# State-space stage: GpSimd multiplies a unit's four states by C in one instruction, not in two of two states each

## The chip, the cores and the metric

One NeuronCore of a Trainium2 chip runs the whole program. The metric is the device time of one execution in microseconds (us). Five engines run their own instruction streams and meet at semaphores: TensorE (PE in the profile), VectorE (DVE), ScalarE (ACT), GpSimd (POOL) and SyncE (SP, which issues DMAs).

## What is computed

A model of two layers on 2 x 4096 tokens of width 512. The change is in its first block, a selective state-space block (Mamba), which is cut here to what the scan needs:

```
h   = silu(causal_conv4(layernorm(x) @ in_proj_hidden))          # 1024 channels
dt, B, C = rms-normed parts of h @ x_proj_w                      # B, C: 16 states per token
dt  = softplus(dt @ dt_proj_w + dt_proj_b)
s_t = exp(dt_t * A) * s_(t-1) + dt_t * h_t * B_t                 # per channel and state
y_t = sum over the 16 states of s_t * C_t
x   = x + ((y + h * D) * silu(gate)) @ out_proj_w
```

A mixing matmul, a linear-attention layer and a routed spline layer follow. They are a stage of their own, which begins when the first has ended.

## The kernel before

**Tiling.** The state-space stage (`mamba_block`) goes through 16 chunks: 8 blocks of T = 512 tokens for each of 2 batch rows. A chunk holds 1024 channels x 16 states x 512 tokens. Channels lie in 8 groups of 128 partitions and states in 4 quarters of 4. A **unit** is one group with one quarter: 128 channels x 4 states x 512 tokens, so 32 units a chunk and 512 in all. The loop over units is `for k in range(U)` in the body of each engine. I call its turn number k of a chunk **step k**.

**What each engine does for unit k.** The order on each engine is written out by hand.

- TensorE, `b_product(k)` (line 737): 16 small matmuls make dt * h * B for the four states in the four PSUM banks `BU`. There is one `BU`, so it waits for `scan_done`, until all four scans of unit k-1 have read it.
- ScalarE (line 501): four exponentials write exp(dt * A) into the slot `s[k % 4]`. They wait for `sum_done`, which tells that the slot's former unit has been summed.
- VectorE (lines 651 to 656): four scans, one for each state, in place in `s[k % 4]`. Then comes `piece(k)`, a part of the work that prepares the next chunk (convolution, norm, softplus, gating), and then a small reduce, which saves the last column and signals `state_saved`.
- GpSimd (line 335): waits for `state_saved` of unit k, multiplies `s[k % 4]` in place by `Cb`, which is C broadcast to all partitions, and signals `z_ready`. It does so in two instructions of two states each.
- TensorE, `y_sum(k_even, part)` (line 754): 8 matmuls with the identity add the products into the PSUM banks `Y`. A call handles two states of an even unit and of the odd unit behind it. `part` 0 takes states 0 and 1, `part` 1 states 2 and 3.
- SyncE (line 219) loads the next `Cb` when `z_ready` tells that the units so far are multiplied.

**The order on TensorE.** In step k it runs `b_product(k)`, then larger pieces for the next or the previous chunk (`before(k)` and `main(k)`: transposes and projections into `PJ`), and one call `sums(k)`. In odd steps (but for k = 11) `sums(k)` comes right after `b_product(k)`. In even steps it comes last, so that `b_product(k+1)` stands right behind it; in step 12 eight transposes stand between. In an even step `sums(k)` is part 0 of the units k-2 and k-1. In an odd step it is part 1 of the units k-3 and k-2. Its wait counts product instructions:

```
pe.wait_ge(z_ready, c * 2 * U + 2 * k - 1 if part == 0 else c * 2 * U + 2 * (k - 1))
```

With two signals a unit, the value 2k-1 is reached when GpSimd has done all of unit k-2 and the first half of unit k-1.

Of the kernel before, what the change touches and what calls it, by code (L numbers as in the profile page):

```python
# [9 lines left out]
ALU = mybir.AluOpType  # L10
# [4 lines left out]
T = 512  # L15
# [6 lines left out]
def wait(eng, sem, value):  # L22

    if not isinstance(value, int) or value > 0:
        eng.wait_ge(sem, value)
# [33 lines left out]
def mamba_block(nc, x, in_w, chan, xproj_w, dt_w, out_w, eye, tokmask, x1):  # L59
# [9 lines left out]
    U = G * NQ  # L69
# [3 lines left out]
    NCH = BATCH * NI  # L73
    SLOTS = 4
# [6 lines left out]
    with ctx:  # L81
        def sb(name, shape, dt=F32):
            return ctx.enter_context(nc.sbuf_tensor(name, shape, dt))
# [4 lines left out]
        def sem(name):  # L88
            return ctx.enter_context(nc.semaphore(name))
# [21 lines left out]
        s = [sb(f"s{i}", [P, 4, T]) for i in range(SLOTS)]  # L111
        Cb = [sb(f"Cb{i}", [P, 4 * T]) for i in range(2)]
# [33 lines left out]
        z_ready, sum_done, y_ready = sem("z_ready"), sem("sum_done"), sem("y_ready")  # L146
# [57 lines left out]
        def _(sp):  # L204
            def held(sem_, value):

                wait(sp, sem_, value)
                sp.sem_inc(sp_steps, 1)
# [8 lines left out]
            def load_c(q, slot):  # L217
                src = bc[slot][4 * (q % NQ):4 * (q % NQ) + 4, :].rearrange("(o n) t -> o (n t)", o=1)
                sp.dma_start(Cb[q % 2][:], src.to_broadcast([P, 4 * T])).then_inc(c_loaded[q % 2], 16)
# [5 lines left out]
            def load_x(ring_, use, period, b_next, i_next, half):  # L225
                held(*ring_.emptied(use, period))
                sp.dma_start(xt[:], x_v[b_next, i_next, :, 2 * half:2 * half + 2, :]).then_inc(x_loaded, 16)
# [6 lines left out]
            def load_res(i_prev, b_prev, c_prev, j):  # L234

                held(x1_stored[j % 2], 16 * (c_prev * 2 + j // 2))
                sp.dma_start(res[:, j % 2, :], x_v[b_prev, i_prev, :, j, :]).then_inc(res_loaded[j % 2], 16)

            def store_x1(i_prev, b_prev, c_prev, j):
                held(x1_ready, c_prev * NT + j + 1)  # L240
                sp.dma_start(x1_v[b_prev, i_prev, j], res[:, j % 2, :]).then_inc(x1_stored[j % 2], 16)

            def body(i, b, c, first, last):
                i_prev, b_prev, c_prev = (i, 0, c - 1) if b else (i - 1, 1, c - 1)
                i_next, b_next = (i + 1, 0) if b else (i, 1)
                for k in range(U):
                    if k == 0:
                        if not last:
                            held(spread_ready, NQ * (c + 1))
                            if first:  # L250
                                load_x(ahead, ("xT", 3), 0, b_next, i_next, 0)
                            else:
                                load_x(steady, ("xT", 3), c - 1, b_next, i_next, 0)
                        if not first:
                            held(bc_stored, 16 * (c + 1))
                            load_res(i_prev, b_prev, c_prev, 0)
                            load_res(i_prev, b_prev, c_prev, 1)
                    if k % 2 == 0:
                        held(z_ready, c * 2 * U + 2 * k)
                        if k // 2 + 1 < U // 2:  # L260
                            load_c(k // 2 + 1, b)
                        elif not last:
                            held(bc_stored, 16 * (c + 2))
                            load_c(0, 1 - b)
                    if not first:
                        if k == 4:
                            store_x1(i_prev, b_prev, c_prev, 0)
                        if k == 6:
                            load_res(i_prev, b_prev, c_prev, 2)
                        if k == 7:  # L270
                            store_x1(i_prev, b_prev, c_prev, 1)
                        if k == 9:
                            load_res(i_prev, b_prev, c_prev, 3)
                        if k == 11:
                            store_x1(i_prev, b_prev, c_prev, 2)
                        if k == 12:
                            store_x1(i_prev, b_prev, c_prev, 3)
                    if k == 9 and not last:
                        load_x(steady, ("xT", 1), c, b_next, i_next, 1)
                    if k == 29 and not last:  # L280
                        store_bc(steady, c, 1 - b)
# [9 lines left out]
        @block.gpsimd  # L291
        def _(pool):
            nc.gpsimd.memset(minus_half[:], -0.5)
            nc.gpsimd.memset(state[:], 0.0)
            nc.gpsimd.memset(hist[:], 0.0)
            pool.drain().then_inc(consts_ready, 1)

            def ln_power(c_next, half):
                wait(pool, stats_ready, 2 * c_next + half + 1)
                nc.gpsimd.tensor_tensor(rstd[:], ve[:], minus_half[:, 0:2], ALU.pow).then_inc(rstd_ready, 1)  # L300

            def ssm_power(c_next):
                wait(pool, ssq_ready, c_next + 1)
                nc.gpsimd.tensor_tensor(rssm.rearrange("p j n -> p (j n)"), ssq.rearrange("p j n -> p (j n)"),
                                        minus_half[:], ALU.pow).then_inc(rssm_ready, 1)

            def spread_b(c_next, nq):
                pool.wait_ge(ssm_ready, c_next + 1)
                lo = RANK + 4 * nq
                nc.gpsimd.tensor_tensor(spread[:, nq], mask[:].unsqueeze(1).unsqueeze(3).to_broadcast([P, TB, 32, 4]),  # L310
                                        ssm[:, :, lo:lo + 4].unsqueeze(2).to_broadcast([P, TB, 32, 4]),
                                        ALU.mult).then_inc(spread_ready, 1)

            ln_power(0, 0)
            ln_power(0, 1)
            ssm_power(0)
            pool.wait_ge(small_loaded, 48)
            for nq in range(NQ):
                spread_b(0, nq)

            def body(i, b, c, first, last):
                for k in range(U):
                    if k == 2 and not last:
                        ln_power(c + 1, 0)
                    if k == 10 and not last:
                        ln_power(c + 1, 1)
                    if k == K_SUMS and not last:
                        ssm_power(c + 1)
                    q = k // 2
                    if k % 2 == 0:  # L330
                        wait(pool, c_loaded[q % 2], 16 * (c * (U // 4) + (q % (U // 2)) // 2 + 1))
                    wait(pool, state_saved, c * U + k + 1)
                    for part in range(2):
                        pair = s[k % SLOTS][:, 2 * part:2 * part + 2, :].rearrange("p n t -> p (n t)")
                        nc.gpsimd.tensor_tensor(pair, pair, Cb[q % 2][:, 2 * part * T:2 * part * T + 2 * T],  # L335
                                                ALU.mult).then_inc(z_ready, 1)
                    if k == 0 and not first:
                        wait(pool, dbu_ready, c * U)
                        spread_b(c, 3)
                    if k in (28, 29, 30) and not last:  # L340
                        nq = k - 28
                        wait(pool, dbu_ready, c * U + 26 + 2 * nq)
                        spread_b(c + 1, nq)

            periods(pool, body)

        @block.scalar
# [317 lines left out]
        def _(pe):  # L665
# [115 lines left out]
            def body(i, b, c, first, last):  # L781
                def sums(k):
                    part = k % 2
                    k_even = (k - part - 2) % U
                    if k < 2 and first:
                        return
                    if k_even % UP == 0 and part == 0:
                        wait(pe, y_ready, c * G + 2 * (k_even // UP))
                        pe.sem_inc(pe_steps, 1)
                        skip_product(k_even // UP, b)  # L790
                    pe.wait_ge(z_ready, c * 2 * U + 2 * k - 1 if part == 0 else c * 2 * U + 2 * (k - 1))
                    pe.sem_inc(pe_steps, 1)
                    y_sum(k_even, part)

# [49 lines left out]
                for k in range(U):  # L844
                    if k % UP == 0:
                        p = k // UP
# [17 lines left out]

            periods(pe, body)
            for part in range(2):
                pe.wait_ge(z_ready, NCH * 2 * U - 1 + part)
                y_sum(U - 2, part)
            pe.wait_ge(y_ready, G * NCH)
            for j in range(NT):  # L870
# [1020 lines left out]
```

## Time and profile before

| | us |
|---|---|
| median of 3 runs | 5543.72 (5543.46 to 5544.86) |
| the profiled execution, its own time | 5545.57 |
| its span, first to last instruction | 5543.6 |

The span begins with some 120 us of loads and the first chunk's preparation. The scans run from 123.2 to about 3793 us, and the second stage takes the rest. A steady chunk takes some 231 us. The chunk read below is the eighth. Its last step before (k = 31 of the seventh) ends at 1732.6 us, and its steps 4, 12, 16, 22 and 28 are looked at.

How to read it: "busy" is time in which an engine executed something. The time named in square brackets in front of an arrow is how long the engine stood idle before the row, and behind the arrow is the instruction that ended the wait. In the timeline, equal instructions that follow each other are one row with their count. TensorE runs an fp32 matmul as two passes here, so `y_sum` shows as x16 and `b_product` as x32. Ends of matmuls are modelled, so I go by their starts.

### The profile page before, as it was taken

To read this page: it belongs to the slowest core of one execution; us is meant where nothing else is said; L and a number is where in the kernel's file an instruction comes from. 1 tells how busy PE (TensorE), PEld (TensorE's weight loads), DVE (VectorE), ACT (ScalarE), POOL (GpSimd) and SP (SyncE) were. 2 spreads that over 40 slices of the span, in tenths; PEclk is the share of its full clock that TensorE was granted. 3 is DMA by queue.
4 is the path that set the end of the run, shared out by engine and by line. 5 is a ranking of instruction groups with operands and counts; after the bars stand their busy time and mean duration, and the time that the engine had idled before them with its cause. 6 is when DMAs were issued, how large, how long until landed. Compare 5 with 4: busy or idle time off the path is not lost. (4 is left out here: it accounts for less than half of the span.)

```text
span 5543.6 us, 108449 instructions
## 1 busy us (share of the span) xinstructions
PE 4955.6 (89%) x41157; PEld 2941.5 (53%) x41157; DVE 4611.2 (83%) x7532; ACT 2636.9 (48%) x4244; POOL 3148.7 (57%) x1611
## 2 busy tenths in 40 slices
PE   6899999999999999999999999974899999999922
PEld 3354444454445444454444444432688888888822
DVE  3988889888898888988889888884688888888888
ACT  3655656556565565655656556551233333333300
POOL 1676766767667676676766767662244444434323
PEclk9999999999999999999999999987899999999955
DMA  2222222212222222222222222223110000101034
GB/s 82 81 96 73 100 79 90 96 73 100 81 89 96 73 100 84 85 97 73 100 85 85 96 73 100 81 88 133 37 31 28 29 29 28 31 26 31 22 124 140
DMA packets 139999, 422.20 MB, mean 76 GB/s; under 512 B 38368, under 2 KB 39904, under 8 KB 106592
## 3 DMA queue, kind: packets, MB, share of 16 engines
q1 hardware_dynamic: 136672, 411.75, 21.1%
q8 instruction: 337, 5.52, 0.4%
q10 hardware_dynamic: 2816, 3.51, 0.2%
q14 instruction: 174, 1.43, 0.1%
HBM read 361.99 MB, written 53.22 MB: 75 GB/s over the span
## 5 line engine op out<-in xcount | busy, mean ns | idle before, releaser
L335 POOL TENSOR_TENSOR s<-s,Cb 128x1024 f32<-128x1024 f32 x1024 | 2395.0, 2360 | 1081.9 <-DVE state L656 1070.4
L651 DVE TENSOR_TENSOR_SCAN s<-s,state,BU 128x512 f32<-128x512 f32 x2048 | 2452.9, 1260 | 423.4 <-PE BU L737 387.1
L501 ACT ACTIVATE s<-dt,ch 128x512 f32<-128x512 f32 x2048 | 1305.6, 712 | 776.3 <-PE Y L754 774.7
L754 PE MATMUL Y<-s,ident 64*64 64x512 f32 x8192 | 1010.7, 609 | 78.5 <-POOL s L335 77.6
L683 PE MATMUL PJ<-xnT,w_in 128*128 128x512 f32 x2048 | 946.9, 606 | 9.0 <-ACT dtuT L367 5.7
L737 PEld LDWEIGHTS BU<-spread,dtuT 32*128 32x128 f32 x16384 | 512.4, 189 | 528.8 <-DVE s L651 403.2
L737 PE MATMUL BU<-spread,dtuT 32*128 32x128 f32 x16384 | 610.9, 286 | 146.4 <-DVE s L651 141.0
L683 PEld LDWEIGHTS PJ<-xnT,w_in 128*128 128x128 f32 x2048 | 370.1, 190 | 479.0 <-issue 424.2
L754 PEld LDWEIGHTS Y<-s,ident 64*64 64x64 f32 x8192 | 279.1, 134 | 572.8 <-issue 535.2
L728 PE MATMUL PJ<-w_out,u 128*128 128x512 f32 x1024 | 471.7, 604 | 8.3 <-ACT xnT L371 6.7
L728 PEld LDWEIGHTS PJ<-w_out,u 128*128 128x128 f32 x1024 | 184.5, 189 | 242.9 <-issue 225.3
L1103 POOL TENSOR_TENSOR x1t<-x1t,bias_b 128x512 f32<-128x512 f32 x64 | 82.8, 1294 | 397.4 <-DVE xa L1286 397.4
L544 DVE SCALAR_TENSOR_TENSOR u<-hid,ch,u 128x512 f32<-128x512 f32 x384 | 287.6, 749 | 19.1
L694 PE MATMUL PJ<-w_xp,u 128*128 128x160 f32 x1024 | 253.0, 404 | 9.6 <-issue 6.5
L694 PEld LDWEIGHTS PJ<-w_xp,u 128*128 128x128 f32 x1024 | 243.1, 329 | 27.2 <-issue 20.8
L1108 POOL TENSOR_TENSOR xf<-xf,gamma_b 128x512 f32<-128x512 f32 x64 | 81.5, 1273 | 305.3 <-DVE xf L1475 305.3
L1484 DVE TENSOR_TENSOR scm<-bank,decay 128x512 f32<-128x512 f32 x256 | 159.0, 684 | 71.1 <-PE bank L1593 71.1
L1554 PE MATMUL bank<-w_high_o,aTs 128*128 128x512 f32 x512 | 179.9, 412 | 0.0
L1116 POOL TENSOR_TENSOR qk_all<-rc,rs 128x512 f32<-128x512 f32 x64 | 82.1, 1283 | 172.1 <-DVE rs L1502 172.1
L367 ACT COPY dtuT<-PJ 128x512 f32<-128x512 f32 x128 | 68.8, 587 | 231.8 <-PE PJ L723 231.8
L1554 PE MATMUL bank<-w_high_f,xaT 128*128 128x512 f32 x512 | 177.1, 407 | 1.5 <-DVE xaT L1291 1.4
L1291 DVE TENSOR_TENSOR xaT<-bank,xaT 128x512 fp32r<-128x512 f32 x64 | 44.2, 691 | 161.2 <-ACT xaT L1158 161.2
(219 smaller groups left out, 7171.7 us busy)
## 6 DMA issues: line engine op xcount, KB each, us to landing
Cb<-bc SPq DMA_DIRECT2D x256, 1024.0 KB, 4.8
res<-in_x SPq DMA_DIRECT2D x64, 256.0 KB, 4.8
x<-res SPq DMA_DIRECT2D x64, 256.0 KB, 5.0
x1t<-x SPq DMA_DIRECT2D x64, 256.0 KB, 2.6
out<-r_t SPq DMA_DIRECT2D x64, 256.0 KB, 2.0
xt<-in_x SPq DMA_DIRECT2D x31, 512.0 KB, 5.7
x_all<-out SPq DMA_DIRECT2D x16, 512.0 KB, 4.2
scm<-out SPq DMA_DIRECT2D x16, 512.0 KB, 4.6
```

The source lines that it names most:

```text
L335: nc.gpsimd.tensor_tensor(pair, pair, Cb[q % 2][:, 2 * part * T:2 * part * T + 2 * T], ALU.mult).then_inc(z_ready, 1)
L501: nc.scalar.activation(s[k % SLOTS][:, n, :], dt[p % 2][:, gi, :], ACT.Exp, scale=ch[:, 2 * p + gi, 7 + 4 * nq + n:8 + 4 * nq + n]).then_i ...
L544: last_ = nc.vector.scalar_tensor_tensor(out, h_[:, tap:tap + T], ch[:, m, tap:tap + 1], out, ALU.mult, ALU.add)
L651: nc.vector.tensor_tensor_scan(s[k % SLOTS][:, n, :], s[k % SLOTS][:, n, :], BU[:, n::4], state[:, b, k, n:n + 1], ALU.mult, ALU.add).then ...
L683: last_ = nc.tensor.matmul(bank[:], w_in[:, kb, lo:lo + P], xnT[:, kb, :], start=(kb == 0), stop=(kb == KB - 1))
L694: last_ = nc.tensor.matmul(bank[:, tb % 2 * SP_:(tb % 2 + 1) * SP_], by_block(u[slot][:, g, :])[:, tb], w_xp[:, g, :], start=(g == 0), sto ...
L728: last_ = nc.tensor.matmul(bank[:], u[slot][:, g, j * P:(j + 1) * P], w_out[:, g, :], start=(g == 0), stop=(g == G - 1))
L737: last_ = nc.tensor.matmul(BU[:, i * T:(i + 1) * T].rearrange("p (t b n) -> p b t n", b=TB, n=4)[:, tb], dtuT[rows, gi, tb, :], spread[row ...
L754: last_ = nc.tensor.matmul(Y[r][y_rows(r, gi), :], ident[rows, rows], s[(k_even + gi) % SLOTS][rows, n, :], start=False, stop=(n == 3 and ...
L1103: nc.gpsimd.tensor_tensor(x1t[s_][:], x1t[s_][:], bias_b[:], ALU.add).then_inc(S["x1b_ready"], 1)
L1484: nc.vector.tensor_tensor(scm[:, r, :, :].rearrange("p k n -> p (k n)"), bank(f"sc{r}")[:], decay[:, r, :, :].rearrange("p k n -> p (k n)" ...
L1554: last_ = nc.tensor.matmul(b_[:], src[part][:, k, :], wt, start=(k == 0 and i == 0), stop=(k == KB - 1 and i == 2))
```

## The change

The product of a unit by C becomes one instruction over 2048 elements a partition. `z_ready` counts once a unit. The waits of TensorE and SyncE are rewritten for that count. In even steps TensorE now waits for all of unit k-1, since a half of a unit no longer has a signal of its own. In odd steps it waits for unit k-2, as before.

```diff
--- before.py
+++ after.py
@@ -256,7 +256,7 @@
                     if k % 2 == 0:
-                        held(z_ready, c * 2 * U + 2 * k)
+                        held(z_ready, c * U + k)
@@ -330,10 +330,8 @@
                     wait(pool, state_saved, c * U + k + 1)
-                    for part in range(2):
-                        pair = s[k % SLOTS][:, 2 * part:2 * part + 2, :].rearrange("p n t -> p (n t)")
-                        nc.gpsimd.tensor_tensor(pair, pair, Cb[q % 2][:, 2 * part * T:2 * part * T + 2 * T],
-                                                ALU.mult).then_inc(z_ready, 1)
+                    whole = s[k % SLOTS][:].rearrange("p n t -> p (n t)")
+                    nc.gpsimd.tensor_tensor(whole, whole, Cb[q % 2][:], ALU.mult).then_inc(z_ready, 1)
@@ -788,7 +786,7 @@
-                    pe.wait_ge(z_ready, c * 2 * U + 2 * k - 1 if part == 0 else c * 2 * U + 2 * (k - 1))
+                    pe.wait_ge(z_ready, c * U + k - (part == 1))
                     pe.sem_inc(pe_steps, 1)
                     y_sum(k_even, part)
@@ -864,7 +862,7 @@
             for part in range(2):
-                pe.wait_ge(z_ready, NCH * 2 * U - 1 + part)
+                pe.wait_ge(z_ready, NCH * U)
                 y_sum(U - 2, part)
```

GpSimd, the first chunk from step 2 on (`rstd` and `xt` are its small instructions for the next chunk's norms, `spread` the broadcast of B). Before:

```order
L300 TENSOR_TENSOR rstd<-ve,minus_half 128x2
L335 TENSOR_TENSOR s<-s,Cb 128x1024 x16
L300 TENSOR_TENSOR rstd<-ve,minus_half 128x2
L335 TENSOR_TENSOR s<-s,Cb 128x1024 x32
L304 TENSOR_TENSOR xt<-xt,minus_half 128x12
L335 TENSOR_TENSOR s<-s,Cb 128x1024 x6
```

And now:

```order
L300 TENSOR_TENSOR rstd<-ve,minus_half 128x2
L334 TENSOR_TENSOR s<-s,Cb 128x2048 x8
L300 TENSOR_TENSOR rstd<-ve,minus_half 128x2
L334 TENSOR_TENSOR s<-s,Cb 128x2048 x16
L304 TENSOR_TENSOR xt<-xt,minus_half 128x12
L334 TENSOR_TENSOR s<-s,Cb 128x2048 x3
```

Nothing changes its place. Every pair of products has become one instruction of twice the size.

TensorE in step 12 of a steady chunk, with its waits (L716 is a projection of `dt`, L676 the transposes of the next input; ISA and REGISTER_ALU are instructions of its sequencer). Before:

```order
L716 MATMUL PJ<-dtnT,w_dt 128x512 [waits proj_taken_dve_steady] x2
L791 REGISTER_ALU
L754 MATMUL Y<-s,ident 64x512 [waits z_ready]
L754 MATMUL Y<-s,ident 64x512 x7
L25 REGISTER_ALU
L25 REGISTER_ALU [waits xn_ready]
L676 MATMUL PJ<-ident,xt 128x128 [waits proj_taken_act_steady]
```

And now:

```order
L714 MATMUL PJ<-dtnT,w_dt 128x512 [waits proj_taken_dve_steady] x2
L752 MATMUL Y<-s,ident 64x512 [waits z_ready]
L752 MATMUL Y<-s,ident 64x512 x7
L25 REGISTER_ALU
L25 REGISTER_ALU [waits xn_ready]
L674 MATMUL PJ<-ident,xt 128x128 [waits proj_taken_act_steady]
```

The matmuls keep their order. The register instruction of line 791, which computed the wait's value, is gone (two line numbers less are the change's own lines), and the wait on `z_ready` has the same place but stands for another event.

## Rows read from the trace of the kernel before

**Rows 1.** The page's busy times: engine, busy us (share of span), instructions.

```profile
PE 4955.6 (89%) x41157; PEld 2941.5 (53%) x41157; DVE 4611.2 (83%) x7532; ACT 2636.9 (48%) x4244; POOL 3148.7 (57%) x1611
```

**Rows 2.** The page's costliest groups: busy us, mean ns | idle before, releaser.

```profile
L335 POOL TENSOR_TENSOR s<-s,Cb 128x1024 f32<-128x1024 f32 x1024 | 2395.0, 2360 | 1081.9 <-DVE state L656 1070.4
L651 DVE TENSOR_TENSOR_SCAN s<-s,state,BU 128x512 f32<-128x512 f32 x2048 | 2452.9, 1260 | 423.4 <-PE BU L737 387.1
...
L754 PE MATMUL Y<-s,ident 64*64 64x512 f32 x8192 | 1010.7, 609 | 78.5 <-POOL s L335 77.6
```

**Rows 3.** Timeline, step 12: start us, duration us, engine, instruction [idle before].

```profile
1816.12 4.68 POOL L335 TENSOR_TENSOR s<-s,Cb 128x1024 f32<-128x1024 f32 x2 [2.06 <-DVE state L656]
...
1818.62 1.95 PE L754 MATMUL Y<-s,ident 64*64 64x512 f32 x16 [1.11 <-POOL s L335]
1820.50 1.09 PE L676 MATMUL PJ<-ident,xt 128*128 128x128 f32 x8
1821.52 1.17 PE L737 MATMUL BU<-spread,dtuT 32*128 32x128 f32 x32
...
1822.85 4.80 DVE L651 TENSOR_TENSOR_SCAN s<-s,state,BU 128x512 f32<-128x512 f32 x4 [1.32 <-PE BU L737]
```

**Rows 4.** Timeline, step 4 and the start of step 5.

```profile
1762.27 4.68 POOL L335 TENSOR_TENSOR s<-s,Cb 128x1024 f32<-128x1024 f32 x2 [1.65 <-DVE state L656]
...
1765.30 1.95 PE L754 MATMUL Y<-s,ident 64*64 64x512 f32 x16
1767.18 1.17 PE L737 MATMUL BU<-spread,dtuT 32*128 32x128 f32 x32
...
1768.91 4.79 DVE L651 TENSOR_TENSOR_SCAN s<-s,state,BU 128x512 f32<-128x512 f32 x4
```

**Rows 5.** Timeline, step 16 and the start of step 17.

```profile
1848.02 1.95 PE L754 MATMUL Y<-s,ident 64*64 64x512 f32 x16 [0.18 <-POOL s L335]
...
1850.20 1.17 PE L737 MATMUL BU<-spread,dtuT 32*128 32x128 f32 x32 [0.23 <-DVE s L651]
...
1852.83 3.61 DVE L651 TENSOR_TENSOR_SCAN s<-s,state,BU 128x512 f32<-128x512 f32 x3
```

**Rows 6.** Timeline, step 22 to the start of step 24.

```profile
1894.62 1.95 PE L754 MATMUL Y<-s,ident 64*64 64x512 f32 x16 [0.48 <-POOL s L335]
1896.79 1.17 PE L737 MATMUL BU<-spread,dtuT 32*128 32x128 f32 x32 [0.23 <-DVE s L651]
...
1905.16 1.17 PE L737 MATMUL BU<-spread,dtuT 32*128 32x128 f32 x32
...
1906.48 2.45 DVE L651 TENSOR_TENSOR_SCAN s<-s,state,BU 128x512 f32<-128x512 f32 x2 [2.31 <-PE BU L737]
```

**Rows 7.** Timeline, step 28 and the start of step 29.

```profile
1940.47 1.95 PE L754 MATMUL Y<-s,ident 64*64 64x512 f32 x16 [1.43 <-POOL s L335]
...
1943.03 1.17 PE L737 MATMUL BU<-spread,dtuT 32*128 32x128 f32 x32 [0.61 <-DVE s L651]
...
1944.35 2.45 DVE L651 TENSOR_TENSOR_SCAN s<-s,state,BU 128x512 f32<-128x512 f32 x2 [1.19 <-PE BU L737]
```

**Rows 8.** One line's instructions on GpSimd: duration ns min/median/max, first and last start.

```profile
L1108 POOL TENSOR_TENSOR xf<-xf,gamma_b x64: 1261/1273/1303, 3973.9 to 5277.2; 128x512 f32<-128x512 f32 x64
L300 POOL TENSOR_TENSOR rstd<-ve,minus_half x32: 695/696/711, 20.0 to 3424.3; 128x2 f32<-128x2 f32 x32
```

**Rows 9.** Busy times in a stretch: from:to, us, PE busy (instructions), granted clock, DMA.

```profile
230.00:3660.00 3430.00, 3255.25 (x28232) 1.00 0.25 88
...
187.00:190.00 3.00, 3.00 (x40) 0.50 0.02 5
```

**Rows 10.** Timeline, TensorE: first chunk, last chunk, and step 18 of the eighth.

```profile
186.84 2.09 PE L737 MATMUL BU<-spread,dtuT 32*128 32x128 f32 x32 [3.04 <-DVE s L651]
...
3740.99 3.69 PE L754 MATMUL Y<-s,ident 64*64 64x512 f32 x16 [1.45 <-POOL s L335]
...
1864.14 1.95 PE L754 MATMUL Y<-s,ident 64*64 64x512 f32 x16 [0.65 <-POOL s L335]
```

## The prediction, made before the result was known

> **What bounds the kernel now.** I read the page's busy times first. TensorE is busy for 89% of the span, VectorE for 83% and GpSimd for 57% [rows 1], so GpSimd as a whole has time to spare and a cheaper product buys nothing by itself. The costliest groups say who waits for whom. VectorE's scans stand idle for 423.4 us, and 387.1 of them end with `b_product`. GpSimd's 1081.9 us of idle time end with the reduce that saves the state, and `y_sum` waited for GpSimd for only 78.5 us [rows 2]. So the state-space stage is set by a loop of TensorE and VectorE: the scans of a unit end, `b_product` of the next unit runs, its scans start. GpSimd hangs on that loop through one thread: in even steps `y_sum` stands ahead of the next `b_product` on TensorE. The timeline shows how tight this thread is. In step 12 the two products start at 1816.12, 4.68 us for both. With 2.36 for one [rows 2] the first half ends at 1818.48, and `y_sum` starts at 1818.62, 0.14 later, while the second half still runs [rows 3]. This shape, `y_sum` on the heels of the first half, is there in six even steps of a steady chunk: 12, 16, 18, 20, 22 and 28.
>
> **What the change costs, part by part.**
>
> *The product.* Two instructions of 1024 elements go, one of 2048 comes. The trace has none of that size. From 512 to 1024 elements the time grows from 1.273 [rows 8] to 2.360 [rows 2], 1.087 for 512. Two more such steps give 2.360 + 2 x 1.087 = 4.53 us. The long end is the pair as it is, 4.68 [rows 3]. For the short end, all 0.696 us of the two-element instruction [rows 8] would be overhead that is paid once less: 3.98. I take 4.53, the value nearest to the rows of this same operation. GpSimd gains 0.15 us a unit, which lies in its idle time and costs or brings nothing.
>
> *The signal.* In an even step `y_sum` could start when half of unit k-1 was multiplied. Now it starts 0.14 after the whole. Where it followed the first half, it comes 4.53 - 2.36 = 2.17 us later. What is queued behind it on TensorE is `b_product` of the next unit, and VectorE's scans wait for that. Three things can cover the 2.17: work ahead of `y_sum` that ends later than the signal anyway, idle time of TensorE between `y_sum` and `b_product`, and a scan that starts later than `b_product`'s result because VectorE still has its piece to do. `y_sum` holds TensorE for 1.88 us (1765.30 to 1767.18 [rows 4]), and a scan can start 1.33 after the start of its `b_product` (1821.52 to 1822.85 [rows 3]).
> - Step 12: only eight transposes stand between, TensorE isn't idle, and the scans wait for `b_product` [rows 3]. No cover: 2.17.
> - Step 16: `b_product` starts at 1850.20, 0.30 after `y_sum` lets go; the scan starts at 1852.83, 1.30 later than it could [rows 5]. 2.17 - 0.30 - 1.30 = 0.57. The convolutions on VectorE are that cover. Steps 18 and 20 read alike: three times 0.57 = 1.71.
> - Step 22: idle 1896.79 - 1896.50 = 0.29. Then TensorE runs without a gap to the `b_product` of step 24 at 1905.16, for which VectorE waits 2.31 us [rows 6]. So all that is left arrives there: 1.88.
> - Step 28: idle 1943.03 - 1942.35 = 0.68, and the scan waits for `b_product` [rows 7]: 1.49.
> - Step 4: `y_sum` now starts at 1765.30, held by the projections. The product's new end is 1762.27 + 4.53 = 1766.80, so the sum moves to 1766.94, by 1.64. The scan has 0.40 of cover (1768.91 against 1768.51) [rows 4], but TensorE finds no idle time in the next two steps and hands the rest over there: 1.6.
> - The other even steps: most have a `y_sum` that starts late enough behind larger work, and I put 0.5 on the lot.
>
> Sum of the waits: 2.17 + 1.71 + 1.88 + 1.49 + 1.6 + 0.5 = 9.35 us a chunk, 150 us in 16 chunks.
>
> *TensorE's clock.* Today it is granted 1.00 from 230 to 3660 us, thus 2.4 GHz throughout [rows 9]. In the first chunk, where TensorE has less to do, it stood idle for 3.04 us, and then the `b_product` at 186.84 took 2.09 us [rows 10] instead of 1.17 [rows 3]; the granted clock from 187 to 190 is 0.50, which is 1.2 GHz [rows 9]. In the last chunk a `y_sum` behind 1.45 us of idle time took 3.69 instead of 1.95 [rows 10], 1.74 more. The change makes the idle time ahead of `y_sum` longer: 1.11 + 2.17 = 3.28 in step 12 [rows 3], 1.43 + 2.17 = 3.60 in step 28 [rows 7], 0.65 + 2.17 = 2.82 in step 18 [rows 10], 0.48 + 2.17 = 2.65 in step 22 [rows 6]. Two of these are longer than the 3.04 that went ahead of a fall. So I expect falls in every steady chunk: surely those two, and of the two or three stretches between 2.3 and 2.9 half. That is 3.5 falls, each of which costs one `y_sum` at half speed, 1.74, in places whose cover is spent already: 6.1 us a chunk. The first and the last chunk fall today, so 14 are counted: 85 us. The Trainium skill, TensorE: Matmul & The Clock Gate, Part 1, says the same in general: an idle array is throttled, and activity releases it. By that rule the sum is 235; by this trace's steady stretch alone, in which no clock fell, it would be 150.
>
> *What costs nothing.* SyncE's wait stands for the same event as before. The odd steps wait for the same product as before, one step old. One register instruction a step goes from TensorE's sequencer, which works ahead while matmuls run; if it were never hidden, it would give back less than the 0.14 between signal and sum. The exponentials wait for the sums of odd steps, which move only as `b_product` does; the scans waited for `b_product` in 387.1 of their 423.4 idle us [rows 2], so there is little that late exponentials held up. The Trainium skill, GPSIMD Engine Reference, section 2.1, speaks for the change: every Pool instruction pays a software dispatch of tens of cycles. By that rule 512 dispatches are saved; they lie in GpSimd's idle time, and the sum stays what it is.
>
> Sum against the profiled execution: 5545.57 + 150 + 85 = 5780.6. It lies 1.85 above the median, so the forecast for the median is 5543.72 + 235 = 5779.
>
> **The rivals.**
> - *The clock holds.* The idle stretches grow, but TensorE is busy enough around them, and it stays at 2.4 GHz, as it does today in the whole steady stretch. For it: 3255 of those 3430 us are busy [rows 9]. Against it: 3.60 and 3.28 are longer than 3.04. Then only the waits count: 5694. With the short product, 3.98 instead of 4.53, each of seven steps gains 0.55, 3.9 a chunk and 62 in all: 5632. With the long one, 4.68, they lose 0.15 each, 17 in all.
> - *The wait is covered.* If VectorE's pieces covered the later `b_product` in all steps as in step 16, a chunk would lose some 0.5 us and the kernel 8: 5552, within 0.2%. Against it: in steps 12, 24 and 28 to 29 the scans wait for `b_product` today [rows 3, 6, 7].
> - *Faster: the big product is as quick as one half.* If GpSimd's time hung on the instruction and not on its elements, the whole unit would be ready when its first half is today. The point is 2.36 us. Below it the even sums start earlier, and what is to be had is at most the 78.5 us in which `y_sum` waited for GpSimd [rows 2]; at 1.9 us, 0.46 in steps 12, 22 and 28, that is 1.4 a chunk and 22 in all: 5522. Against it: 1273 ns for 512 elements and 2360 for 1024.
> - *More falls.* All five stretches of step 12, 16, 18, 22 and 28 fall, 5 x 1.74 = 8.7 a chunk, 122 in all, with the long product 17 more: 5544 + 150 + 122 + 17 = 5833.
>
> **How the numbers follow.** The waits with falls of the clock, some 5750 to 5835, get 0.70; the waits with a clock that holds 0.26; covered 0.02; faster 0.02. The range goes from 5680, which takes in the clock that holds with a product somewhat shorter than I think (5694 - 14), to 5840, just above all falls with the long product. A measurement here can tell about 0.2%, 11 us, from no change. Faster by more than that: 0.02. Within: 0.02. Slower: 0.96.
>
> **What would show it.** Right: line 334 with 512 instructions of some 4.5 us; in step 12 `y_sum` 0.14 after the product's end, and VectorE's idle time ahead of the scans up from 423 us by more than 100; a steady chunk of some 246 us instead of 231; a granted clock below 1.00 from 230 to 3660 us, with `y_sum` rows of over 3 us. Clock wrong: those rows stay at 1.95 and the clock at 1.00, with a chunk of 240 us. The second stage should keep its length. The forecast fails altogether if the scans of steps 13, 24 and 29 start no later behind their predecessors than now, or if the product takes less than 3 us.

## The result, and the profile after

| | before | after |
|---|---|---|
| median, us | 5544.29 (4 runs, 5543.46 to 5545.29) | 5792.06 (4 runs, 5781.93 to 5794.45) |
| ratio | | 1.0442, 95% interval 1.0427 to 1.0458 |
| profiled execution, its own time | 5545.57 | 5781.93 |
| its span | 5543.6 | 5780.1 |
| stretch of the scans, from the timeline | 123.2 to 3789.8 | 122.0 to 4027.7 |

The change makes the kernel 4.4% slower: 247.8 us by the medians, where 235 were forecast. The profiled execution of the changed kernel is the fastest of its four, 10.1 us below their median, so the two profiles are only 236.4 us apart. All of that lies in the state-space stage: its scans take 3905.7 us instead of 3666.6, 239.1 more, and the rest of the program is 2.6 us shorter.

The page's busy times, as in [rows 1]:

```profile
PE 5026.5 (87%) x41157; PEld 2974.3 (51%) x41157; DVE 4610.1 (80%) x7532; ACT 2639.1 (46%) x4244; POOL 3073.2 (53%) x1099
```

VectorE and ScalarE do the same work as before in a longer span. GpSimd has 512 instructions less and is busy for 75.5 us less, 0.15 for each unit. TensorE has the same number of instructions and is busy for 70.9 us more: some of them ran slower.

The page's costliest groups, which answer to [rows 2] (busy us, mean ns | idle before, releaser):

```profile
L334 POOL TENSOR_TENSOR s<-s,Cb 128x2048 f32<-128x2048 f32 x512 | 2319.6, 4530 | 1389.7 <-DVE state L654 1386.0
...
L649 DVE TENSOR_TENSOR_SCAN s<-s,state,BU 128x512 f32<-128x512 f32 x2048 | 2453.9, 1260 | 663.4 <-PE BU L735 636.0
...
L752 PE MATMUL Y<-s,ident 64*64 64x512 f32 x8192 | 1066.1, 638 | 311.5 <-POOL s L334 311.3
```

`y_sum` waits for GpSimd 311.3 us instead of 77.6. The scans wait for `b_product` 636.0 us instead of 387.1, which is 248.9 more, the size of the loss. The matmuls of `y_sum` have a mean of 638 ns instead of 609.

Step 12 of the eighth chunk in the timeline, which answers to [rows 3] (start us, duration, engine, instruction, idle before in square brackets):

```profile
1917.78 4.52 POOL L334 TENSOR_TENSOR s<-s,Cb 128x2048 f32<-128x2048 f32 x1 [2.21 <-DVE state L654]
...
1922.45 3.64 PE L752 MATMUL Y<-s,ident 64*64 64x512 f32 x16 [3.28 <-POOL s L334]
1926.03 1.09 PE L674 MATMUL PJ<-ident,xt 128*128 128x128 f32 x8
1927.05 1.17 PE L735 MATMUL BU<-spread,dtuT 32*128 32x128 f32 x32
...
1928.38 4.80 DVE L649 TENSOR_TENSOR_SCAN s<-s,state,BU 128x512 f32<-128x512 f32 x4 [5.18 <-PE BU L735]
```

The product ends at 1922.30 and `y_sum` starts 0.15 later. It used to start 2.50 after the product's start and now starts 4.67 after it: 2.17 later. TensorE stands idle for 3.28 us instead of 1.11. Then the sum takes 3.64 us instead of 1.95, since the clock has fallen. The scans behind it waited for 5.18 us instead of 1.32, and 3.86 is 2.17 + 1.69.

Steps 18 (with the `b_product` of step 19) and 28 (with that of step 29) of the same chunk, from the same timeline:

```profile
1972.61 2.65 PE L752 MATMUL Y<-s,ident 64*64 64x512 f32 x16 [2.37 <-POOL s L334]
1975.19 2.08 PE L735 MATMUL BU<-spread,dtuT 32*128 32x128 f32 x32
...
2053.40 3.69 PE L752 MATMUL Y<-s,ident 64*64 64x512 f32 x16 [3.43 <-POOL s L334]
2057.02 2.09 PE L735 MATMUL BU<-spread,dtuT 32*128 32x128 f32 x32
2059.26 3.62 DVE L649 TENSOR_TENSOR_SCAN s<-s,state,BU 128x512 f32<-128x512 f32 x3 [5.17 <-PE BU L735]
```

Here the `b_product` behind the sum runs at half speed too, 2.09 us instead of 1.17. In step 18 the idle time before the fall is 2.37 us, less than the 3.04 of [rows 10].

Busy times in four stretches (from:to, us, then PE, PEld, DVE, ACT and POOL busy, granted clock, DMA share, GB/s), which answer to [rows 9]:

```profile
230.00:3660.00 3430.00, 3131.14 (x26564) 1551.76 (x26560) 2820.02 (x3431) 1906.29 (x2786) 2136.50 (x547) 0.98 0.23 83
...
1924.00:1928.00 4.00, 4.00 (x52) 2.13 (x44) 0.00 (x0) 2.35 (x4) 3.81 (x1) 0.76 0.81 295
2052.00:2056.00 4.00, 2.60 (x13) 0.88 (x16) 2.05 (x3) 1.91 (x4) 3.08 (x2) 0.53 0.44 121
...
3878.00:4034.00 156.00, 90.73 (x975) 41.59 (x977) 105.69 (x110) 57.13 (x89) 93.02 (x21) 0.74 0.18 65
```

The granted clock is 0.98 where it was 1.00, and 0.53 around the sum of step 28. Between its two levels, 1.2 and 2.4 GHz, a mean of 0.98 still means that most of the time passes at the high one. The last row is the last chunk; in the kernel before, a stretch around it has 0.81.

**How the losses are counted below.** From the timelines of two kernels I take the time from the end of one unit's scans to the end of the next unit's, and subtract the kernel before. The means are over chunks 3 to 15. For a whole chunk I add them up. A "fall" is a stretch in which the granted clock is 0.50, counted in chunks 2 to 15. The kernel before has none there, the changed kernel 37, and the clock is low for 164 us in all: 12 falls near step 12, 3 in step 15, 12 near step 18, 1 in step 23 and 9 in step 28. By these counts chunks 2 to 15 take 201.2 us more (14.4 each, 230.5 becomes 244.9), the first chunk 14.6 and the last 23.2. In the first and the last chunk the clock is low for some time in both kernels: for 27.3 and 47.8 us before, for 41.0 and 75.1 after.

### The profile page after: what moved, and what is told of

It is laid out like the page before. It is cut to its first block and busy times, and to the rows that moved or that the text cites. A ratio compares the mean times of both kernels' runs of the same rounds, so it can differ in the third digit from the quotient of the medians.

```text
span 5780.1 us, 107565 instructions
## 1 busy us (share of the span) xinstructions
PE 5026.5 (87%) x41157; PEld 2974.3 (51%) x41157; DVE 4610.1 (80%) x7532; ACT 2639.1 (46%) x4244; POOL 3073.2 (53%) x1099
## 5 line engine op out<-in xcount | busy, mean ns | idle before, releaser
L334 POOL TENSOR_TENSOR s<-s,Cb 128x2048 f32<-128x2048 f32 x512 | 2319.6, 4530 | 1389.7 <-DVE state L654 1386.0
L649 DVE TENSOR_TENSOR_SCAN s<-s,state,BU 128x512 f32<-128x512 f32 x2048 | 2453.9, 1260 | 663.4 <-PE BU L735 636.0
L752 PE MATMUL Y<-s,ident 64*64 64x512 f32 x8192 | 1066.1, 638 | 311.5 <-POOL s L334 311.3
L735 PEld LDWEIGHTS BU<-spread,dtuT 32*128 32x128 f32 x16384 | 530.4, 195 | 477.4 <-issue 260.6
L752 PEld LDWEIGHTS Y<-s,ident 64*64 64x64 f32 x8192 | 293.3, 138 | 822.3 <-issue 784.2
L735 PE MATMUL BU<-spread,dtuT 32*128 32x128 f32 x16384 | 630.2, 292 | 79.8 <-DVE s L649 77.1
L408 ACT ACTIVATE dt<-PJ,ch 128x512 f32<-128x512 f32 x128 | 85.8, 683 | 208.4 <-PE PJ L714 208.2
```

Source lines behind the costliest of these rows:

```text
L334: nc.gpsimd.tensor_tensor(whole, whole, Cb[q % 2][:], ALU.mult).then_inc(z_ready, 1)
L408: nc.scalar.activation(dt[p % 2][:, gi, :], PJ[ring_.bank(use)][:], ACT.Identity, bias=ch[:, 2 * p + gi, 6:7]).then_inc(ring_.taken["act"], 1)
L649: nc.vector.tensor_tensor_scan(s[k % SLOTS][:, n, :], s[k % SLOTS][:, n, :], BU[:, n::4], state[:, b, k, n:n + 1], ALU.mult, ALU.add).then ...
L735: last_ = nc.tensor.matmul(BU[:, i * T:(i + 1) * T].rearrange("p (t b n) -> p b t n", b=TB, n=4)[:, tb], dtuT[rows, gi, tb, :], spread[row ...
L752: last_ = nc.tensor.matmul(Y[r][y_rows(r, gi), :], ident[rows, rows], s[(k_even + gi) % SLOTS][rows, n, :], start=False, stop=(n == 3 and ...
```

## The experiments

The theory that the prediction leaves has two halves. (A) Even steps lose the half-unit signal, so `y_sum` comes 2.17 us later and `b_product` and the scans behind it come late wherever nothing covers it. (B) The longer idle time of TensorE makes its clock fall, and the sums and products after it run at half speed. The rivals: the loss comes from the form of the big instruction (its size on GpSimd, its use of memory beside the scans) rather than from its signal; or all of the loss is waiting, and the slow rows lie in time that is covered anyway.

### The wait alone: e1_whole_wait

The kernel before, with both instructions of two states. Only TensorE waits for the second half in even steps.

```diff
-  pe.wait_ge(z_ready, c * 2 * U + 2 * k - 1 if part == 0 else ...)
+  pe.wait_ge(z_ready, c * 2 * U + 2 * k if part == 0 else ...)
```

> The kernel before with its two products a unit; TensorE's wait in even steps is for both (2k in place of 2k-1). If the loss is the wait, this kernel has all of it, and a little more than the change: the pair ends 4.68 us after its start, the one product 4.53, so seven even sums a chunk come 0.15 later still, about 17 us in all: 5800 to 5825, with the clock falling as in the changed kernel. If the large instruction itself does the harm (holding something that VectorE or TensorE needs), this kernel has no large instruction and stays at 5544.

Measured: 5841.59, ratio 1.0529 (1.0511 to 1.0546) to 5544.71 of the same chip. That is 297 us, more than the change itself loses, and above what was expected. The page's costliest groups:

```profile
L335 POOL TENSOR_TENSOR s<-s,Cb 128x1024 f32<-128x1024 f32 x1024 | 2392.4, 2358 | 1385.4 <-DVE state L656 1379.3
...
L651 DVE TENSOR_TENSOR_SCAN s<-s,state,BU 128x512 f32<-128x512 f32 x2048 | 2453.9, 1261 | 718.3 <-PE BU L737 693.5
...
L754 PE MATMUL Y<-s,ident 64*64 64x512 f32 x8192 | 1100.8, 656 | 338.2 <-POOL s L335 337.9
```

The small instructions keep their 2.36 us, and the idle times of the changed kernel appear all the same. So the signal carries the loss. The whole unit is ready 0.15 us later than with one instruction, and the clock falls 58 times instead of 37, low for 232 us: that is the piece I had put too low. The changed kernel waits for the whole unit too and is some 50 us faster (5792.06): its product ends 0.15 us sooner, and its clock falls less often.

### Which units: e2_even_units_one and e3_odd_units_one

In an even step k the half signal stands for unit k-1, which is odd. Here the kernel before gets one instruction over four states, with two counts at its end, for the even units alone (shown) or for the odd units alone (mirrored).

```diff
+  if k % 2 == 0:
+      whole = s[k % SLOTS][:].rearrange("p n t -> p (n t)")
+      nc.gpsimd.tensor_tensor(whole, whole, Cb[q % 2][:], ALU.mult).then_inc(z_ready, 2)
-  for part in range(2):
+  for part in range(2 if k % 2 else 0):
```

> The kernel before, but the units of even number are multiplied in one instruction of 2048 elements (which counts 2 on the signal), those of odd number in two as before. The even sum of step k follows the first half of unit k-1, which is odd, so by the theory of the wait nothing on the path moves: 5544, within 0.2%, the clock at 1.00 in the steady stretch. If each large instruction costs something by itself, half of the change's loss is here: about 5668.

> The mirror of the kernel with even units in one instruction: odd units in one, even units in two. By the theory of the wait this has the whole loss of the change: 5785 to 5800. If each large instruction costs by itself: about 5668, the same as its mirror.

Measured: even units 5542.99, ratio 0.9996 (0.9986 to 1.0006), no fall. Odd units 5807.87, ratio 1.0474 (1.0457 to 1.0492), 42 falls; some 8 us above the range that was expected. The page's costliest groups, even units alone:

```profile
L338 POOL TENSOR_TENSOR s<-s,Cb 128x1024 f32<-128x1024 f32 x512 | 1197.4, 2360 | 592.4 <-DVE state L659 592.4
L335 POOL TENSOR_TENSOR s<-s,Cb 128x2048 f32<-128x2048 f32 x256 | 1160.4, 4533 | 526.0 <-DVE state L659 517.3
...
L654 DVE TENSOR_TENSOR_SCAN s<-s,state,BU 128x512 f32<-128x512 f32 x2048 | 2453.1, 1261 | 427.3 <-PE BU L740 395.5
```

And the scans' group where the odd units alone are merged:

```profile
L654 DVE TENSOR_TENSOR_SCAN s<-s,state,BU 128x512 f32<-128x512 f32 x2048 | 2454.0, 1261 | 680.8 <-PE BU L740 648.7
```

The same 256 big instructions of 4533 ns cost nothing in one place and the whole loss in the other. The rival of the instruction's form is out: its size, its duration and its use of memory are the same in both kernels.

### One step, three steps, five steps: e5, e6 and e7

The kernel before, where the wait for the whole unit is set in some even steps only.

```diff
-  ... 2 * k - 1 if part == 0 ...
+  ... 2 * k - (k not in (12,)) if part == 0 ...                # e5
+  ... 2 * k - (k not in (16, 18, 20)) if part == 0 ...         # e6
+  ... 2 * k - (k not in (2, 8, 10, 24, 26)) if part == 0 ...   # e7
```

> The kernel before with its two products; TensorE waits for both in step 12 alone. By the theory of the wait this step has no cover: the even sum moves by 4.68 - 2.36 = 2.32 us and the scans of step 13 with it, 37 us in 16 chunks; and the idle time of 3.4 us ahead of the sum lets the clock fall as it did in the changed kernel, some 1.6 more in most chunks: 5590 to 5608 in all. If the loss of 297 us of the kernel that waits for both everywhere were spread over its 16 even steps alike, one of them would cost 19: 5563.

> The same wait for both products in steps 16, 18 and 20 alone. Each sum moves by 2.32; 0.30 lies in TensorE's idle time and 1.30 behind VectorE's convolution, so each costs 0.72, 2.2 a chunk, 35 us: 5580, and up to 5605 if the clock falls behind the idle time of step 18 (2.97 us). If VectorE's pieces covered nothing, the three would cost 3 x 2.02 = 6.1 a chunk: 5642 and more. Spread alike over the even steps: 5600.

> The same wait for both products in steps 2, 8, 10, 24 and 26 alone, where the even sum starts later than the pair ends today, since larger work stands ahead of it. By the theory nothing moves: 5544, within 0.2%. Spread alike over the even steps: 5 x 19 = 93, so 5637.

| | median | ratio to 5543.84 | chunks 2 to 15 | falls |
|---|---|---|---|---|
| step 12 | 5593.46 | 1.0090 (1.0073 to 1.0106) | +44.1 | 8 |
| steps 16, 18, 20 | 5607.78 | 1.0118 (1.0101 to 1.0134) | +49 | 14 |
| steps 2, 8, 10, 24, 26 | 5551.64 | 1.0014 (1.0004 to 1.0024) | -1.9 | 0 |

Step 12 by itself costs what was expected of it. Steps 16, 18 and 20 cost 28 us more than 5580, the sum without falls, and 3 more than the top of the expected range: step 17 is 1.68 and step 19 1.46 longer, and eight of the falls come before the scans of step 17, where the changed kernel has none. Where the clock didn't fall, steps 17 and 19 are 0.7 us longer each, as worked out from the covers. Step 20 is 0.45 longer and step 21 0.1: part of the wait of step 18 arrives one step later, and little of that of step 20 is left. The third row was expected to show nothing, and in chunks 2 to 15 it does. In the profile the loss lies in the first chunk (+4.4) and the last (+6.4, 4.0 of them in step 27). In the last chunk the projections for a next chunk, which cover the late sum elsewhere, are skipped. The clock has a part in it too: it is low for 61.4 us of the last chunk instead of 47.8, and the sum of step 26 takes 3.69 us there instead of 1.95.

### The clock held up by extra matmuls: e4_fill and e8_fill_more

The changed kernel with matmuls repeated ahead of the waiting sums. Each repeat writes what is written again behind it, so the outputs stay. They fill time in which TensorE stood idle. e4 has them in steps 12, 18, 22 and 28. e8, whose diff is shown, adds steps 4 and 14, which is where e4 still had falls behind.

```diff
-def project(ring_, use, period, lo):
+def project(ring_, use, period, lo, again=0):
+    for _ in range(again):
+        nc.tensor.matmul(bank[:], w_in[:, 0, lo:lo + P], xnT[:, 0, :], start=True, stop=True)
...
-for j in range(NT):              # turn_ssm, step 28
+for j in list(range(NT)) * 7:
...
+    for _ in range(3 if gi and p == 2 else 0):      # projection of dt, step 12
+        nc.tensor.matmul(bank[:], w_dt[:, lo:lo + P], dtnT[:], start=True, stop=True)
...
+project(steady, ("gate", m), c, INTER + m * P, {4: 1, 22: 2}.get(k, 0))
+project(steady, ("hid", HID_AT[k]), c, HID_AT[k] * P, {14: 2, 18: 3}.get(k, 0))
```

> The changed kernel with matmuls repeated into the same bank with the same result, in the steps where TensorE would stand idle ahead of the even sum: 3 more of the dt projection in step 12 (2.6 us), 3 and 2 more of a projection in steps 18 and 22, 24 more transposes in step 28 (about 3.1 us). They end before the product does, so the waits keep their length. If the fall of the clock is a term of its own, it is gone: the granted clock is 1.00 in the steady stretch and the time falls by what steps 13, 19 and 29 took beyond their waits, (3.86 - 2.17) + (2.19 - 0.57) + (3.98 - 1.49) = 5.8 us a chunk, 81 us in 14 chunks: about 5711. If the falls are only a companion of the waits, hidden behind them, the time stays at 5792 or rises.

> The changed kernel with the repeated matmuls of the kernel before it in this study, and 2 more in step 14 and 1 more in step 4, where its clock still fell (9 times in 14 chunks). Scans of step 15 took 1.28 us longer there than in the kernel before, and 0.22 was the share of the wait: if the rest is the clock, some 0.8 a chunk goes, 12 us: 5715 to 5722, with the clock at 1.00 in the steady stretch. What is left over the kernel before is then the wait alone, and should be 150 us by the prediction's first sum: 5694 to 5715.

Measured: e4 5730.60, ratio 1.0334 (1.0317 to 1.0351), 9 falls left (31 us low), 7 of them in step 15; with those the run is 20 us above what was expected. e8 5716.48, ratio 1.0310 (1.0293 to 1.0327), no fall in chunks 2 to 15. More work on the busiest engine makes the changed kernel 75.6 us faster. Step 12 of e8 in the timeline:

```profile
1888.92 4.51 POOL L334 TENSOR_TENSOR s<-s,Cb 128x2048 f32<-128x2048 f32 x1 [2.20 <-DVE state L654]
1889.29 2.74 PE L717 MATMUL PJ<-dtnT,w_dt 128*128 128x512 f32 x6
1891.87 1.02 PE L718 MATMUL PJ<-dtnT,w_dt 128*128 128x512 f32 x2
...
1893.58 1.95 PE L756 MATMUL Y<-s,ident 64*64 64x512 f32 x16 [0.69 <-POOL s L334]
...
1897.81 4.79 DVE L649 TENSOR_TENSOR_SCAN s<-s,state,BU 128x512 f32<-128x512 f32 x4 [3.40 <-PE BU L739]
```

The sum starts 4.66 after the product's start, as in the changed kernel, so the wait is fully there. It takes 1.95, and the scans wait 3.40 instead of 5.18. The page's groups of e8:

```profile
L649 DVE TENSOR_TENSOR_SCAN s<-s,state,BU 128x512 f32<-128x512 f32 x2048 | 2453.3, 1260 | 588.4 <-PE BU L739 535.8
...
L756 PE MATMUL Y<-s,ident 64*64 64x512 f32 x8192 | 1014.0, 610 | 132.4 <-POOL s L334 131.9
```

The mean matmul of `y_sum` is back at 610 ns, with 609 in [rows 2]. This run divides the loss: 5792.06 - 5716.48 = 75.6 us go with the falls that the extra matmuls took away, 5716.48 - 5543.84 = 172.6 us stay. In chunks 2 to 15, where no fall is left, what stays is 130.9 us, the waits alone. In the first and the last chunk it is 11.9 and 24.3 us, and the clock is still low there for 34.1 and 68.3 us instead of 27.3 and 47.8, so some of those 36 us is the clock's. How much, no run shows. The rival in which the slow rows lie in covered time is out.

### Other places for the sum of step 12: e9, e10 and e11

Can the product in one instruction be had at a lower price? In e9, on the changed kernel, `sums(12)` goes behind `b_product(13)`, so that the scans of step 13 don't hang on it. In e10, shown below, the eight transposes of step 12 go ahead of the sum.

```diff
     before(k)
-    if k == 12:
-        sums(k)
     main(k)
-    if not sums_first and k != 12:
+    if not sums_first:
         sums(k)
```

> The changed kernel; the even sum of step 12 is issued behind b_product of step 13 in place of ahead of it. The late signal then holds up nothing that VectorE waits for in step 13, where the changed kernel loses 3.8 us a chunk. TensorE has the sum's 1.88 us to do in step 13 as well, with a projection of 3.4 behind it, so the b_product of step 14 comes some 1 to 1.5 later than today. Net 2.5 to 3 us a chunk better than the change: 5740 to 5755. If it weren't the place of the sum in TensorE's queue but GpSimd's later result as such, nothing would be won: 5792.

> The changed kernel; in step 12 the eight transposes (1.02 us) stand ahead of the sum in place of behind it, so they run in the 3.28 us in which TensorE waits for the product. The wait alone gives back 1.0 a chunk: 5776. If the shorter idle time, some 2.2, also keeps the clock up, step 13 goes from 3.8 us over the kernel before to 1.2, and 2.6 in 14 chunks come back: about 5752.

> The same exchange in the kernel before: transposes ahead of the sum in step 12. There TensorE waits only 1.11 us, and the transposes can't all start at once, since their bank is freed by a copy of ScalarE. At best 0.5 us a chunk is won, 8 us: 5536 to 5545. It would be a version that is no slower than either kernel.

Measured: e9 5766.82, ratio 1.0402 (1.0386 to 1.0418), a miss by 12 us. e10 5776.66, ratio 1.0420 (1.0404 to 1.0436). The sum of step 12 in the timeline of e10:

```profile
1919.45 1.95 PE L752 MATMUL Y<-s,ident 64*64 64x512 f32 x16 [1.82 <-POOL s L334]
```

The idle time ahead of that sum is 1.82 instead of 3.28 and the sum is fast, yet the kernel gains 15 us and not 40. It comes out at the 5776 that a shorter wait alone was to give, but not in that way: step 13 is 2.02 us shorter than in the changed kernel (28 us in 14 chunks), and steps 15 and 23 are 0.63 and 0.73 longer. The falls moved: e10 has 43, of which 5 are near step 12, 8 in step 15, 9 near step 18, 8 in step 23 and 13 in step 28. e9 has 45, with 10 near step 13, 11 near step 18, 10 in step 23 and 14 in step 28. In e9 steps 13 and 14 together are 2.0 us cheaper than in the changed kernel, less than the 2.5 to 3 expected, steps 15 to 17 save another 0.8, and steps 23 and 29 give back 1.35 a chunk (2.05 - 0.92 and 3.31 - 3.09). The idle time ahead of the sum of step 22 is the same in the changed kernel, e9 and e10, from 2.0 to 2.5 us in every chunk from 2 to 15, and the falls behind it number 1, 10 and 8. So the idle time ahead of a sum doesn't decide by itself whether the clock falls.

e11 makes the exchange of e10 in the kernel before: 5539.80, ratio 0.9990 (0.9981 to 0.9999) to 5544.02. A chunk is 0.44 us shorter. It is the best version that I saw, within the 0.2% that a measurement here can tell from no change, so I call it no slower and no more.

## Why the prediction was right

**The product.** 4.53 us were worked out from 1.273 and 2.360, and 4.530 is the mean. The time grows with the elements, and one instruction less saves 0.15 us. That is 75.5 us of busy time on GpSimd, and it doesn't show in the kernel's time. The Trainium skill, GPSIMD Engine Reference, section 2.1, says that each instruction on GpSimd pays a software dispatch, and the trace agrees that something is saved for each.

**The waits.** e8, where the clock stays up in chunks 2 to 15, shows them without the falls, in us a chunk:

| | predicted | e8 |
|---|---|---|
| step 12 (scans of 13) | 2.17 | 2.16 |
| step 16 (scans of 17) | 0.57 | 0.0 |
| step 18 (scans of 19 and 20) | 0.57 | 0.58 + 0.45 = 1.03 |
| step 20 (scans of 21) | 0.57 | 0.03 |
| step 22 (scans of 23 and 24) | 1.88 | 0.81 + 1.07 = 1.88 |
| step 28 (scans of 29) | 1.49 | 1.33 |
| step 4 (scans of 5 and 6) | 1.6 | 1.09 + 0.39 = 1.48 |
| the other steps | 0.5 | 1.45 |
| sum | 9.35 | 9.35 |

Chunks 2 to 15 of e8 take 130.9 us more, 9.35 each, the forecast to the digit. The mechanism earned most of that, and luck the rest: steps 12, 22, 28 and 4 came out within 0.2 us each, but steps 16 and 20 cost next to nothing, step 18 nearly twice its share, and the others three times theirs. Of the 1.45, 0.97 comes with step 14 (scans of 15 and 16: 0.41 + 0.56) and 0.63 with step 30 (scans of the next step 0); step 31 is 0.15 shorter. Neither step was run alone; before the change their sums start 2.89 and 4.06 us after the product does, so they too are held up by a product that takes 4.53. e7 shows only that steps 2, 8, 10, 24 and 26 are covered in a steady chunk.

The piece that the prediction's three covers lack is an earlier delay. Steps 14 to 17 of the eighth chunk of e8, from the timelines of TensorE and VectorE:

```profile
1909.86 1.95 PE L756 MATMUL Y<-s,ident 64*64 64x512 f32 x16 [0.25 <-POOL s L334]
...
1921.11 4.79 DVE L649 TENSOR_TENSOR_SCAN s<-s,state,BU 128x512 f32<-128x512 f32 x4 [0.50 <-PE BU L739]
...
1925.36 1.95 PE L756 MATMUL Y<-s,ident 64*64 64x512 f32 x16 [0.78 <-POOL s L334]
...
1928.57 4.79 DVE L649 TENSOR_TENSOR_SCAN s<-s,state,BU 128x512 f32<-128x512 f32 x4
```

The late sum of step 14 (first row) makes the scans of step 16 late (second row: 0.50 us of idle time where the kernel before has none; the step is 0.56 longer), while GpSimd's product of unit 15 starts no later for it. So the sum of step 16, which waits for that product, waits 0.78 us here and a median of 2.17 in e6, where step 14 isn't touched, and the scans of step 17 don't wait (last row). The 0.45 that step 18 hands to the scans of step 20 covers step 20 in the same way.

**The first and the last chunk.** "150 us in 16 chunks" took them as steady ones, and the clock term counted 14 chunks since "The first and the last chunk fall today". Both were too low. In the changed kernel these two cost 14.6 + 23.2 = 37.8 us instead of 18.7, and the clock is low in them for 41 us longer than before. The last chunk has no next chunk to prepare: TensorE's projections, the cover in steps 24 and 26, aren't there.

**The clock.** "So I expect falls in every steady chunk: surely those two, and of the two or three stretches between 2.3 and 2.9 half." The mechanism was right, as e8 shows. The count was too high: 37 falls in 14 chunks are 2.6 a chunk, not 3.5, and step 12 and step 28 are not sure (12 and 9 of 14). The price of one was a little low: a fall slows the `b_product` behind the sum as well where it lasts, 2.09 against 1.17. From chunk 2 to 15 the clock costs 201.2 - 130.9 = 70.3 us, 1.9 for each fall instead of 1.74, where 85 were forecast. The Trainium skill, TensorE: Matmul & The Clock Gate, Part 1, says that activity releases the throttle, and e8 agrees: with more matmuls the clock is granted in full from chunk 2 to 15, and 75.6 us come back.

**The sum.** In the profiles the waits of chunks 2 to 15 came out as forecast, their clock 15 us lower, the first and the last chunk 19 higher and the rest of the program 2.6 lower: 236.4 us where 235 were forecast. Two errors of opposite sign nearly cancel, which is luck. Of the 13 us by which the forecast for the median was short, the other 12 or so are the distance of the profiled executions from the medians, 10.1 us in the changed kernel and 1.85 in the one before.

**The rivals.** The clock that holds, 5694, was not this kernel; with extra matmuls it comes near it, at 5716, and 17.5 of the 22 us between them are the first and the last chunk. The covered wait is what e7 has in its five steps and what e2 has in all, since there no even sum waits longer. A product as quick as its half is refuted by 4530 ns. More falls, 5833, is near to what e1 did with the long product, 5842 with 58 falls.

## What to carry to other kernels

Before two instructions are merged, look at who counts them: where the consumer stands on its engine ahead of the work of the bounding loop, that loop can pay for the producer's whole second half, while the saved overhead may lie in idle time. Take each place where the consumer waits, subtract what covers it in that step and what an earlier delay covers already, and treat the first and last rounds of the loop by themselves, since what covers a wait is often the next round's work. On TensorE add the clock: here, with idle stretches of 2.0 to 3.5 us ahead of the sums, matmuls at half speed came on top of the wait, and useful or even repeated matmuls in such a gap are worth a trial.

## What the runs showed of the hardware that I had not expected

- The clock can fall after idle times well under the 3.04 us of [rows 10]: after 2.37 in step 18 of the changed kernel, and in three of 14 chunks after 1.98 or 1.99 ahead of the sum of step 14. In e6 the sum of step 16 took 2.60 us instead of 1.95 behind an idle time of 2.50, and the `b_product` behind it 2.09. The same idle time in the next chunk may pass without a fall: step 28 has 9 falls in 14 chunks, with 3.37 to 3.46 us in every one.

```profile
1872.69 2.60 PE L754 MATMUL Y<-s,ident 64*64 64x512 f32 x16 [2.50 <-POOL s L335]
1875.23 2.09 PE L737 MATMUL BU<-spread,dtuT 32*128 32x128 f32 x32
```

(Timeline of e6, TensorE, steps 16 and 17 of the eighth chunk.)

- The count of falls reacts strongly to small shifts. With a product 0.15 us longer (e1) it went from 37 to 58, and moving one sum (e9, e10) raised it to 45 and 43, at other steps. What decides between a fall and none at a given idle time was not measured and stays open.
- Repeated matmuls on the busiest engine shortened the program: in e8 TensorE is busy for 111.8 us more than in the changed kernel (5138.3 against 5026.5), and the program takes 75.6 us less.
